# The mixture of Kronecker experts in layer 0: activated values reordered on GpSimd, a straight-line opening, wider one-hot tables, and a residual that moves

## The reference

```python
def kmoe(x_flat, W_router, A, B, scale, bias, d_in1, d_in2, d_out1, d_out2, top_k):
    logits = x_flat @ W_router.T                      # 64 experts
    vals, idx = jax.lax.top_k(logits, top_k)          # top 2
    probs = jax.nn.softmax(vals, axis=-1)
    xs = x_flat.reshape(-1, d_in1, d_in2)
    Ag = A[idx]; Bg = B[idx]
    Y = jnp.einsum('nkoi,nij,nkpj->nkop', Ag, xs, Bg)
    out = jnp.einsum('nkop,nk->nop', Y, probs).reshape(-1, d_out1 * d_out2)
    return out * scale + bias
h = kmoe(x_flat, W_up, A_up, B_up, scale_up, bias_up, 32, 32, 64, 64, 2)
h = jax.nn.gelu(h, approximate=False)                 # 448 rows of 64 x 64
y = kmoe(h, W_down, A_down, B_down, scale_down, bias_down, 64, 64, 32, 32, 2)
```

## Time and profile before

| | |
|---|---|
| runs | 3529.81, 3537.49, 3544.87 us |
| profiled execution, span | 3536.8 us |
| TensorE busy | 3161.7 us (89%) |
| VectorE busy | 1799.0 us (51%) |
| ScalarE busy | 1187.0 us (34%) |
| GpSimd busy | 928.6 us (26%) |
| mean granted TensorE clock | 0.948 |
| this stage, first transpose to last update of x | 1001.3 to 1333.4 us |

### The profile page before, as it was taken

How to read it: one execution, slowest core, us unless ns; L and a number is a source line. 1 busy time by engine, 2 the same in 40 slices (tenths; PEclk the granted TensorE clock), 3 DMA queues, 4 the chain that set the end, 5 groups by cost and what they waited for, 6 DMA issues and landing times. The chain is left out here.

```text
span 3536.8 us, 75093 instructions
## 1 busy us (share of the span) xinstructions
PE 3161.7 (89%) x30356; PEld 2187.3 (62%) x30356; DVE 1799.0 (51%) x4527; ACT 1187.0 (34%) x2326; POOL 928.6 (26%) x773
## 2 busy tenths in 40 slices
PE   8997999999977887879778999779997999989989
PEld 3434555555666774657544555479997885566656
DVE  8896544543233363443486666543333763355543
ACT  1222333333223333222225555422222562244433
POOL 1002433432000000324417787611111210104001
PEclk9998999999988998989988999989999999999989
DMA  5223000001033010544601110078886300021100
GB/s 158 65 75 83 9 17 10 9 9 27 25 56 24 4 40 15 142 122 148 193 9 44 31 30 26 22 274 331 325 326 238 113 2 13 29 72 49 53 14 18
DMA packets 173983, 287.23 MB, mean 81 GB/s; under 512 B 79184, under 2 KB 144261, under 8 KB 164338
## 3 DMA queue, kind: packets, MB, share of 16 engines
q1 hardware_dynamic: 166194, 262.48, 24.0%
q0 software_dynamic: 7488, 20.46, 1.7%
HBM read 244.49 MB, written 28.48 MB: 77 GB/s over the span
## 5 line engine op out<-in xcount | busy, mean ns | idle before, releaser
L2667 PE MATMUL ps<-L_ffn_xsT,arena 128*128 128x128 f32 x2584 | 303.8, 276 | 1.1 <-DVE L_ffn_xsT L2466 0.6
L2667 PEld LDWEIGHTS ps<-L_ffn_xsT,arena 128*128 128x128 f32 x2584 | 295.8, 192 | 4.5 <-DVE L_ffn_xsT L2466 3.3
L162 POOL TENSOR_TENSOR rstd<-nsc,mhalf 112x4 f32<-112x4 f32 (+2 forms) x24 | 39.2, 1635 | 900.8 <-DVE nsc L155 899.8
L842 POOL TENSOR_TENSOR L_xattn_rn<-L_xattn_ss,mhalf 125x16 f32<-125x16 f32 (+1 forms) x64 | 185.6, 2901 | 258.6 <-DVE L_xattn_ss L905 258.6
L3348 POOL TENSOR_TENSOR L_xattn_pT<-L_xattn_pT,L_xattn_keep 125x678 int32<-125x678 int32 x128 | 190.2, 1507 | 72.1 <-ACT L_xattn_pT L3603 72.1
L2565 ACT ACTIVATE L_ffn_silu<-ps,arena 128x128 f32<-128x128 f32 x280 | 102.9, 368 | 269.4 <-PE ps L2667 253.7
L2475 DVE SCALAR_TENSOR_TENSOR L_ffn_hT<-ps,arena,L_ffn_silu 128x128 f32<-128x128 f32 x280 | 97.9, 350 | 154.9 <-ACT L_ffn_silu L2565 154.9
L1019 PE MATMUL ps<-arena,L_xattn_cT 128*125 128x512 f32 x384 | 166.1, 592 | 0.0
L723 PE MATMUL ps<-L_attn_prod,arena 128*32 128x448 f32 (+28 forms) x672 | 153.6, 492 | 11.9 <-DVE L_attn_prod L523 11.5
L2344 POOL DMA_INDIRECT L_ffn_rows_out<-L_ffn_ys,L_ffn_dest x78 | 79.6, 1020 | 320.0 <-DVE L_ffn_ys L2484 304.4
L2680 PE MATMUL ps<-arena,L_ffn_hT 128*128 128x256 f32 x646 | 153.0, 381 | 7.6 <-ACT L_ffn_ys L2574 7.4
(11 more groups left out here) (604 smaller groups left out, 6830.2 us busy)
## 6 DMA issues: line engine op xcount, KB each, us to landing
arena<-in_L_ffn_up SPq DMA_DIRECT2D x35, 2056.0 KB, 8.0
arena<-in_L_ffn_down SPq DMA_DIRECT2D x35, 1152.0 KB, 8.5
L_xattn_ctxT<-in_ctxT SPq DMA_DIRECT2D x48, 375.0 KB, 3.5
arena<-in_L_ffn_up SPq DMA_DIRECT2D x43, 384.0 KB, 4.5
L_attn_a<-L_attn_skew SPq DMA_DIRECT2D x16, 784.0 KB, 5.2
L_xattn_ctx<-in_ctx SPq DMA_DIRECT2D x30, 375.0 KB
arena<-L_xattn_kp SPq DMA_DIRECT2D x64, 93.8 KB, 3.3
L_xattn_mask<-in_mask SPq DMA_DIRECT2D x32, 164.1 KB, 8.4
```

Source lines behind the costliest of these rows:

```text
L842: nc.gpsimd.tensor_tensor(rn[0:r, i], ss[0:r, i], core.mhalf[0:r, 0:H], ALU.pow).then_inc(po_r.step("root", i), 1)
L2667: ins = nc.tensor.matmul(ps[:, 2 + b % 4, half * TS:(half + 1) * TS], self.up(i % WU, k, half * HM + m), xsT[:, i % 2, k], start=(k == 0), ...
```

## The change

Six edits, all in `L0Kron`. In the changed file the lines of this class stand up to 41 lower.
- Opening: xn is gone; TensorE transposes y itself. The loops are written out, with two PSUM pairs for transposes and two banks for logits, so that TensorE turns group c + 1 before it makes the logits of group c. ScalarE's copy to xT puts the columns of each residue together, so that the stationary operand of the logits is contiguous.
- Routing: `pick(0)` starts when the logits of groups 0 and 1 are kept; `pick(1)` moves behind the fourth turn of a_up0, `weigh(1)` behind its last.
- `spread` holds 128 columns (the 64 experts twice), and one transpose replaces a pair of matmuls. `iota` is loaded twice as wide.
- GpSimd copies each GELU result to `turned_h`, with the pairs contiguous for each f; w0 and w1 read it. Chunk 0's copy lies in the half of h that chunk 1 fills later, chunk 1's in y and xs (two instructions a turn).
- `residual(0)` moves from before b_dn1 to behind z1 on VectorE.
- GpSimd's last `norm_pool` stands behind these copies.

```diff
-        self.iota = a.load(every(d["iota"][0:E], self.P), self.P, E)
+        self.iota = a.take(self.P, 2 * E)
+        for half in range(2):
+            a.loads.append((self.iota[:, half * E:(half + 1) * E], every(d["iota"][0:E], self.P)))
...
+        turned_h = [[by_f(flat[:, CG * F:2 * CG * F], F)],
+                    [by_f(core.y[:, :, :].rearrange("p b c -> p (b c)")[:, 0:CG * F // 2], F // 2), by_f(self.xs.rearrange("p g n -> p (g n)"), F // 2)]]
...
-        spread = rest.take(P, K, K * C, E)
+        spread = rest.take(P, K, K * C, 2 * E)
...
         def _(pool):
             norm_pool(core, norm)
+            for q in range(CHUNKS):
+                if q == 1:
+                    pool.wait_ge(rows_out, DMA)
+                    pool.wait_ge(pe_t.sem, pe_t.at(first["u1"] + INNER - 1))
+                for t in range(INNER):
+                    pool.wait_ge(ac_h.sem, ac_h.at(q, "gelu", t))
+                    for i, to in enumerate(turned_h[q]):
+                        f = F // len(turned_h[q])
+                        ins = nc.gpsimd.tensor_copy(to[:, :, 16 * t:16 * t + 16], h[:, q * CG + 16 * t:q * CG + 16 * t + 16, i * f:(i + 1) * f].rearrange("p g f -> p f g"))
+                    ins.then_inc(po_h.step("turned", t), 1)
             norm_pool(core, lead, 0, U)
...
             def normalise(c):
-                for u in range(U):
-                    normed(core, xn[:, u], U * c + u).then_inc(ve.step("xn", u), 1)
...
-            with dve.Fori(1, NCH) as c:
-                dve.wait_ge(pe.sem, pe.at(c - 1, "xT", KD - 1))
-                core.stand(dve)
+            for c in range(1, NCH):
                 normalise(c)
-            dve.wait_ge(ac.sem, ac.at(NCH - 1, "lg"))
...
+            dve.wait_ge(ac_l.sem, ac_l.at(1, "lg"))
             pick(0, lg[:, 0:C])
             weigh(0, None)
-            pick(1, lg[:, C:2 * C])
...
-            residual(0)
             for t in range(GATHER):
                 gathered_dn("b_dn1", t)
             ended("z1", 1)
+            residual(0)
...
         def _(act):
+                    nc.scalar.copy(xT[c % 2][:, k].rearrange("p (j n) -> p n j", j=8), ps[:, 2 * (c % 2) + k, 0:N4].rearrange("p (n j) -> p n j", j=8)).then_inc(ac_x.step("xT", k), 1)
...
+            keep_turned(0)
+            keep_turned(1)
+            keep_logits(0)
+            keep_turned(2)
+            keep_logits(1)
+            keep_turned(3)
             exp(0)
+            keep_logits(2)
+            keep_logits(3)
             turned("t_up0", 0)
...
         def _(ten):
-                            ins = nc.tensor.matmul(ps[0:P, 2, r * E:(r + 1) * E], xT[:, k, 4 * r + q:N4:8], self.wup[:, KD * q + k, :],
+                            ins = nc.tensor.matmul(ps[0:P, 4 + c % 2, r * E:(r + 1) * E], xT[c % 2][:, k, j * P:(j + 1) * P], self.wup[:, KD * q + k, :],
...
-                            for half in range(2):
-                                ins = nc.tensor.matmul(ps[half * E:(half + 1) * E, even(n) + w, at:at + P], spread[:, w, k * C + c, :], core.ident[0:P, 0:P], start=True, stop=True)
+                            ins = nc.tensor.transpose(ps[:, even(n) + w, at:at + P], spread[:, w, k * C + c, :], core.ident[0:P, 0:P])
...
-                ten.wait_ge(ac_h.sem, ac_h.at(q, "gelu", INNER - 1))
+                ten.wait_ge(po_h.sem, po_h.at(q, "turned", INNER - 1))
...
-                            ins = nc.tensor.matmul(ps[m * E:(m + 1) * E, even(n) + r, 0:CG], self.wdn[p, f + m, :], h[p, q * CG:(q + 1) * CG, f + m],
+                            ins = nc.tensor.matmul(ps[m * E:(m + 1) * E, even(n) + r, 0:CG], self.wdn[p, f + m, :], hT(f + m)[p],
```

More of the change, by code:

```diff
@@ L1257, in weigh @@
                     dve.wait_ge(pe_t.sem, pe_t.at(first[used]))
-                wide = lambda t: t[:, :, :].rearrange("p k n -> p (k n)").unsqueeze(2).to_broadcast([P, K * C, E])
-                nc.vector.tensor_tensor(spread[:, 1], self.iota.unsqueeze(1).to_broadcast([P, K * C, E]), wide(at), ALU.is_equal).then_inc(ve_r.step("plain"), 1)
+                wide = lambda t: t[:, :, :].rearrange("p k n -> p (k n)").unsqueeze(2).to_broadcast([P, K * C, 2 * E])
+                nc.vector.tensor_tensor(spread[:, 1], self.iota.unsqueeze(1).to_broadcast([P, K * C, 2 * E]), wide(at), ALU.is_equal).then_inc(ve_r.step("plain"), 1)
                 dve.wait_ge(ve_r.sem, ve_r.at(i, "plain"))
@@ L1332, in _ @@
                 gathered_up("a_up0", t)
-                if t == 2:
-                    weigh(1, "t_up0")
+                if t == 3:
+                    dve.wait_ge(ac_l.sem, ac_l.at(NCH - 1, "lg"))
+                    pick(1, lg[:, C:2 * C])
+            weigh(1, "t_up0")
             inner("u0", 0)
@@ L1376, in _, with keep_turned, keep_logits @@
         def _(act):
[L1377 removed]
+            def keep_turned(c):
+                if c >= 2:
+                    act.wait_ge(pe_l.sem, pe_l.at(c - 2, "lg"))
                 for k in range(KD):
[L1379 to L1382 removed]
+                    act.wait_ge(pe_x.sem, pe_x.at(c, "xT", k))
+                    nc.scalar.copy(xT[c % 2][:, k].rearrange("p (j n) -> p n j", j=8), ps[:, 2 * (c % 2) + k, 0:N4].rearrange("p (n j) -> p n j", j=8)).then_inc(ac_x.step("xT", k), 1)
+            def keep_logits(c):
+                act.wait_ge(pe_l.sem, pe_l.at(c, "lg"))
+                nc.scalar.copy(lg[:, 2 * c:2 * c + 2, :].rearrange("p c e -> p (c e)"), ps[0:P, 4 + c % 2, 0:2 * E]).then_inc(ac_l.step("lg"), 1)
             def exp(i):
@@ L1460, in _, with turn @@
             ten.wait_ge(run.arrived, run.loads)
-            with ten.Fori(0, NCH) as c:
+            def turn(c):
+                if c >= 2:
+                    ten.wait_ge(ac_x.sem, ac_x.at(c - 2, "xT", KD - 1))
                 for k in range(KD):
@@ L1471, in _ @@
                         for k in range(KD):
-                            ins = nc.tensor.matmul(ps[0:P, 2, r * E:(r + 1) * E], xT[:, k, 4 * r + q:N4:8], self.wup[:, KD * q + k, :],
+                            j = 4 * r + q
+                            ins = nc.tensor.matmul(ps[0:P, 4 + c % 2, r * E:(r + 1) * E], xT[c % 2][:, k, j * P:(j + 1) * P], self.wup[:, KD * q + k, :],
                                                    start=(q == 0 and k == 0), stop=(q == 3 and k == KD - 1))
-                ins.then_inc(pe.step("lg"), 1)
+                ins.then_inc(pe_l.step("lg"), 1)
+            turn(0)
+            for c in range(NCH):
+                if c + 1 < NCH:
+                    turn(c + 1)
+                first_logits(c)
             def banks_free(n):
@@ L1498, in gather_up @@
                     banks_free(n)
+                    if n == 2:
+                        ten.wait_ge(ac_l.sem, ac_l.at(NCH - 1, "lg"))
                     if t == 0:
```

26 lines of the change are left out of this document (16 added, 10 removed).

## The result

| | median us | lowest to highest | ratio to before, 95% interval |
|---|---|---|---|
| before, same chip | 3538.6 (4 runs) | 3529.81 to 3544.87 | |
| changed kernel | 3507.47 (4 runs) | 3501.37 to 3511.47 | 0.9914 [0.9896, 0.9932] |

The kernel is 31.1 us faster; 35.1 were forecast. The profiled execution of the changed kernel is the longest of the four (3511.47 us, span 3509.7, mean clock 0.948 as before), so its span is only 27.1 under that of before. From the first transpose of this stage to the first of the next it goes from 332.9 to 299.6 us (-33.2); ahead of the stage 1.8 are gained, and in the untouched stages behind it 7.9 are lost.

What follows compares the result with a forecast made beforehand. It took the stage, 332 us of 3536.8, to be TensorE's, with losses in the opening, instruction issue, strided sums and a wait for VectorE. Terms summed to -35.1 us: from the median 3537.5 to 3502.4, range 3488 to 3524.

Steps and rivals of the forecast that it cites:

- Opening (-9.1): Stage start through t_up0 and a_up0: a_up0 begins 10.3 us earlier, 1.2 given back beside row loads; together -9.1 us.
- u0 (0): TensorE's block behind a_up0: no change forecast, 0 us.
- b_up0 (0): TensorE's block behind t_up1: no change forecast, 0 us.
- t_up1 (-2.0): Block t_up1: 48 records less at the slow rate of 43 ns, -2.0 us.
- t_dn0 (-2.5): Block t_dn0: 48 records fewer, no issue gap, y1 able to begin earlier; -2.5 us, bounds -1.3 and -3.2.
- w0 (-8.2): Sums w0 behind a_up1: 7.0 us for 16.4, less 1.2 for instructions that had piled up; -8.2 us.
- w1 (-9.3): Sums w1: 7.0 us for 16.6, -9.6, with 0.3 of wait for GpSimd's copies; -9.3 us.
- v0 (+0.3): Block v0 loses the instructions that piled up during w1: +0.3 us.
- b_dn0 (+1.0): Block b_dn0, where z0 waits for VectorE: `weigh(3)` grows by 1.0, so +1.0 us.
- Residual (-5.3): VectorE's residual of chunk 0 leaves b_dn1: z1 starts 5.3 us earlier, nothing given back, at worst 1 us.
- clock and supply eat part: Rival: lower clock and late instructions in opening, a_up0 and w0 leave -26.8 us, 3511 us; chance 0.20.
- My last sign of being wrong: In the stages not touched: the prediction is wrong if one changes by more than 3 us.

Runs made afterwards that it cites:

- the means: Block times averaged over two profiles of the kernel before and three of the changed kernel: all blocks of the stage 329.4 to 298.1 us.
- the pair: The first profile of the kernel before and that of the changed kernel: all blocks of the stage 332.9 to 299.6 us.
- the first group: Runs on one chip; the changed kernel again against the kernel before: median 3506.71 us against 3530.35, ratio 0.9941.
- the third: Third group of runs, on one chip; changed kernel against the kernel before: median 3537.69 us against 3560.14, ratio 0.9929.
- the second group: Runs on one chip: kernel before 3569.47 us; changed kernel with residual back 3539.41, logits' operand strided again 3533.81, narrow one-hot table 3540.09.

## Why the prediction was right, and where its terms were off

The mechanisms held: contiguous sums at 258 ns, no wait for GpSimd, fewer instructions in the turns, a residual that mostly hides. That the total came within 4 us of 35 is in part luck. In the means w0 was 3.5 us short, a_dn1 and v1 cost 2.3 that no term held and the residual was 1.1 short; b_up0 and the blocks without a row gave back 3.4 that nobody forecast.

*Opening (-9.1).* Right in mechanism, 2 to 3 us too small. The start of a_up0 moved by 9.8 us against the stage's start, 10.3 was the sum. On the way two errors cancel. I kept the end of GpSimd's power at 1006.7 and so had group 1's logits over 14.7 us behind the stage's start; four normalisations less stand ahead of the power, it ended at 1003.5, and they were over after 12.9. I put the exponential with its wait at 0.5; VectorE waits 2.04 us, for 1.28 of it ScalarE loads a table, which before the change was done ahead of the need. The table was ready after 19.9 us, as forecast. t_up0 took 1.96 us for its 16 records at a granted clock of 0.50, not 1.1. The sets of logits I put at 2.7 are 3.4 (first, mostly half clock) and 2.0. The 1.2 taken back for more of a_up0 beside the loads did not come there: a_up0 itself became 2.3 us shorter in the means.

*u0 (0) and b_up0 (0).* u0 is +2.6 in the means, +3.8 in the pair, about what a_up0 saved: the two together take 42.0 and 45.0 us before and 44.4, 42.8 and 44.0 after. The row loads are not beside it (DMA share 0.03 in its first 6 us). Its first 6 us hold 194 to 230 records where they held 300 and 252; that a supply of piled-up instructions is missing there is my reading, not shown. With u0 taken in, the opening is -9.4 in the means. b_up0 gave back 2.1 and 5.6, which I had not forecast; it scatters from 16.3 to 20.6 with the same kernel, so these runs don't tell what of it belongs to the change.

*t_up1 (-2.0), t_dn0 (-2.5).* -2.1 and -2.7; with the narrow table put back alone they return, by 2.1 to 2.4 and by 2.6.

*w0 (-8.2).* This is the term that was mis-sized, in both its parts. The sums were to shrink by 9.4, to 7.0 us, and 1.2 were to be given back for the instructions that pile up during slow sums, taken from the one row of u1 with 158 records. The sums shrank by 7.8 in the means and 8.2 in the pair, to 8.5 to 9.1 us, with 1.53 us of waiting for instructions in the rows above. u1 and f0 gave back 3.1 and 4.1, so the term is -4.7 and -4.1. The strided sums say so from the other side: u1 gets 2.9 us shorter when w0 is slow.

*w1 (-9.3).* -9.0. The blocks around it are bound by their arithmetic, so there is no supply to run short of, and TensorE did not wait for GpSimd. A turn costs 2.0 us at chunk 0 and 2.2 at chunk 1, 2.3 was taken. The copy's stride costs GpSimd twice the 0.97 ns a value of a contiguous one; it costs TensorE 2.4 times. By the page "GPSIMD Engine Reference" of the Trainium skill ("Performance pitfalls for Q7 kernels") the estimate was 2.5 us, 0.3 to 0.5 too high; w1's wait that it led to did not come. By the page "SBUF — State Buffer" of the Trainium skill ("Who interferes with whom") nothing was to be added, and the trace agrees: the scaling on VectorE beside the copies takes 1284 ns on average, 1283 before, and GELU on ScalarE 1060 and 1058.

*v0 (+0.3) and b_dn0 (+1.0).* +0.8 and +1.1.

*Residual (-5.3).* -4.9 in b_dn1 and +0.7 in the tail, -4.2 in the means and -3.3 in the pair: 1.1 and 2.0 short, a little more than the 1 us that it was said to cost at worst. On VectorE the last update still waits for its DMA:

```profile
1284.29 1.43 DVE L1333 TENSOR_TENSOR x<-x,y 112x256 f32<-112x256 f32 x4
...
1295.58 1.43 DVE L1333 TENSOR_TENSOR x<-x,y 112x256 f32<-112x256 f32 x4 [2.48 <-DMA y<-L_ffn_y_rows]
```

It starts 27.4 us behind z1's start, 26.3 before the change: the DMA hides nearly all of the moved work, and 2.48 us of wait are left of 3.83.

*What no term held.* a_dn1 +1.0, by a gap of 1.5 us for instructions, and v1 +1.3, by a lower clock at its start. The gap's place goes with the number of instructions ahead of it, its length doesn't; what brings the lower clock is open, since it is there with one long wait and not with two short ones. The rival "clock and supply eat part" named such losses at other places and 8.3 us of them; u1 and f0 took 3 to 4 and u0 2.6 to 3.8, the clock 1.3 at v1, and a_up0 and b_up0 gave about as much back. The lower clock that it feared at w0 did not come, and of the logits only the first set had it.

*The rest of the program.* The stage alone fell by 31.3 us in the means. The medians fell by 31.1 us in the result, 23.6 in the first group and 22.5 in the third. The profiled pair has 7.9 us more in the untouched stages behind; the three variants of the changed kernel in the second group have 3.5 to 8.0 less there than before has in that group. My last sign of being wrong, an untouched stage that changes by more than 3 us, is met twice in the pair: the feed-forward stage of layer 1 goes from 215.9 to 221.1 us and the cross attention of layer 2 from 429.6 to 432.7. Neither follows the change: the first is 213.0 in the repeat of the changed kernel, the second 433.1 in the repeat of the kernel before. The sign was set within the scatter. Whether the change costs a few microseconds outside its stage stays open.

## What to carry to other kernels

Before a slow block's time is booked as a gain, look at the block behind it: if that one waits for "issue", its instructions may have come in during the slow block, and here about a third to a half of the gain went back; a block between arithmetic-bound neighbours (w1) kept it but for 0.8 us in v0. Where a matmul's moving operand steps through memory, let an idle engine reorder it, and price that copy by its own stride. Work that an engine does while another's banks are full goes behind the last block, if a transfer is waited for there anyway.

## What the runs showed of the hardware

- A stream of 64x64 matmuls with 112 moving float32 values 256 bytes apart takes 64 ns a record, 432 ns from start to end of one, and 26 ns and 258 ns with contiguous values. Accumulation has no part in it (429 ns without). A stationary operand with a 32-byte step: 113 against 62 ns a record, and 3.68 us a set at a granted clock of 0.50 as against 3.62 at 1.00; with a contiguous one 3.37 us at 0.57 and 1.99 at 1.00.
- GpSimd copies 1024 values a partition, read 256 bytes apart, in 1997 to 2040 ns in the mean of a profile, and 512 in 1082 to 1147; ScalarE copies 448 values in 534 ns straight and 1021 ns when it writes them strided.
- In blocks that wait for "issue" TensorE began 128 matmul records each 3.3 to 4.0 us. Most of the waits stand 127 or 128 records apart, 256 instructions with the weight loads, and another number of instructions ahead moved one of them out of a block (a_dn1, narrow table). Beside row loads (DMA share 1.7) one block stood 4.33 us for the next.
- The same waits did not bring the same clock. Behind waits of 1.52 and 1.05 us the granted clock was 0.58 for 4 us, behind 1.42 and 1.05 us it stayed 1.00; behind one wait of 2.04 us it was 1.00 in one kernel and 0.50 for 3.3 us in another.
- ScalarE loaded a table for 1.28 us ahead of the stage's first exponential.
